# Two layers of triangle multiplication: masking the finished operands instead of the gates, and a step's stages spread over one more tick

## The reference

```python
# layer 0
z_norm = layer_norm(z, ln_w, ln_b)
m = mask[..., None]
a = (z_norm @ W_ap + b_ap) * sigmoid(z_norm @ W_ag + b_ag) * m
b = (z_norm @ W_bp + b_bp) * sigmoid(z_norm @ W_bg + b_bg) * m
z = z + (einsum('bikc,bkjc->bijc', a, b) @ W_z + b_z)
# layer 1, no mask
x = layer_norm(z, ln1_w, ln1_b)
left, right = sigmoid(x @ left1) * (x @ left2), sigmoid(x @ right1) * (x @ right2)
p = layer_norm(einsum('nsre,nkre->nske', left, right), ln2_w, ln2_b)
out = z + (p @ out_w) * sigmoid(x @ gate)
```

## The kernel before, in words

| stage | ticks | contents | us from the span's start |
|---|---|---|---|
| A | 54 | a z step each, from tick 6 on one half each (0 to 47) | 0 to 247 |
| B | 8 | two halves each (48 to 63), spill | 247 to 291 |
| C | 16 | contraction 0, the last 12 z steps (52 to 63) | 291 to 344 |
| D | 16 | an x step and two halves of layer 0 each | 344 to 447.8 |
| E | 16 | contraction 1 | 447.8 to 482 |
| F | 16 | as D | 482 to 582.7 |
| G | 16 | contraction 2 | 582.7 to 615 |
| H | 16 | an x step each | 615 to 689 |
| I | 16 | contraction 3 | 689 to 716 |
| J | 32 | an x step every second tick, two halves of layer 1 each | 716 to 838 |
| K | 16 | contraction 4 | 838 to 872 |
| L | 16 | a p step and two halves each | 872 to 944 |
| rest | | contraction 5, as L, contraction 6, 16 p steps, contraction 7, 16 p steps | 944 to 1225 |

## Time and profile before

### The profile page before, as it was taken

How to read it: one execution, slowest core, us unless ns; L and a number is a source line. 1 busy time by engine, 2 the same in 40 slices (tenths; PEclk the granted TensorE clock), 3 DMA queues, 4 the chain that set the end, 5 groups by cost and what they waited for, 6 DMA issues and landing times.

```text
span 1225.6 us, 26377 instructions
## 1 busy us (share of the span) xinstructions
PE 900.5 (73%) x9820; PEld 849.1 (69%) x9820; DVE 807.3 (66%) x1883; ACT 583.7 (48%) x834; POOL 690.2 (56%) x441
## 2 busy tenths in 40 slices
PE   1546555467867689676967888888998999956965
PEld 1445454467867579665955888888898999946854
DVE  4888898945658851888167347662597299089097
ACT  1566666653935443455334445553454355333333
POOL 2576777766658851888045213331486188178097
PEclk9876667787988989999988899999999999989989
DMA  2334357776876733665766425676486288866156
GB/s 71 110 106 130 110 146 233 225 237 237 293 218 200 211 103 100 190 196 175 245 210 182 137 78 175 204 260 243 127 305 205 81 293 285 260 219 224 44 190 206
DMA packets 173238, 228.72 MB, mean 187 GB/s; under 512 B 11064, under 2 KB 109624, under 8 KB 171064
## 3 DMA queue, kind: packets, MB, share of 16 engines
q1 hardware_dynamic: 173112, 227.04, 59.4%
HBM read 134.73 MB, written 92.27 MB: 185 GB/s over the span
## 4 chain that ended last, share of the span: by engine, by line
PE 28%; DVE 26%; POOL 19%; issue 17%; ACT 4%; DMA 3%; SPq 2%; DVEq 0%; POOLq 0%; ACTq 0%
PE bank L918 18%; POOL rstd L511 13%; DVE stats L762 7%; DVE xc L795 6%; POOL sig L504 5%; DVE lhs L745 3%; PE ps_w L948 3%; PE bank L902 2%; DVE xc L787 2%; PE bank L903 2%; DVE var L770 2%; POOL xc L523 2%; DMA chunk<-xt 1%; DVE rhs L745 1%; PE ps_x L959 1%
## 5 line engine op out<-in xcount | busy, mean ns | idle before, releaser
L511 POOL TENSOR_TENSOR rstd<-var,minus_half 128x8 f32<-128x8 f32 x192 | 377.3, 1966 | 375.1 <-DVE var L770 375.0
L918 PE MATMUL bank<-rhs,lhs 128*128 128x128 f32 x2048 | 245.6, 283 | 15.5 <-DVE rhs L745 9.0
L504 POOL TENSOR_TENSOR sig<-sig,masks 128x512 f32<-128x512 f32 x128 | 182.6, 1433 | 128.4 <-ACT sig L569 127.5
L569 ACT ACTIVATE sig<-bank 128x512 f32<-128x512 f32 x256 | 153.1, 598 | 212.0 <-PE bank L903 202.0
L918 PEld LDWEIGHTS bank<-rhs,lhs 128*128 128x128 f32 x2048 | 241.0, 198 | 16.5 <-DVE rhs L745 9.5
L959 PE MATMUL ps_x<-ident_b,split 128*128 128x128 bf16 x1024 | 101.1, 257 | 142.9 <-DVE split L802 142.8
L795 DVE TENSOR_TENSOR xc<-xc,rstd 128x504 f32<-128x504 f32 (+1 forms) x192 | 161.1, 839 | 62.3 <-POOL xc L523 35.0
L902 PE MATMUL bank<-w_lhs,chunk 128*128 128x128 bf16 x1024 | 157.1, 242 | 51.7 <-DVE lhs L745 37.9
L902 PE MATMUL bank<-w_rhs,chunk 128*128 128x128 bf16 x1024 | 158.7, 245 | 40.4 <-DVE rhs L745 29.6
L959 PEld LDWEIGHTS ps_x<-ident_b,split 128*128 128x128 bf16 x1024 | 78.0, 116 | 158.5 <-DVE split L802 134.6
L948 PE MATMUL ps_w<-w_out,opair 128*128 128x128 f32 x1024 | 152.0, 296 | 39.1 <-DVE split L809 35.4
(11 more groups left out here) (83 smaller groups left out, 1348.7 us busy)
## 6 DMA issues: line engine op xcount, KB each, us to landing
xt<-xt SPq DMA_DIRECT2D x96, 512.0 KB, 4.4
chunk<-xt SPq DMA_DIRECT2D x80, 512.0 KB, 4.4
xin<-in_x_dram SPq DMA_DIRECT2D x128, 256.0 KB, 3.0
x<-xin SPq DMA_DIRECT2D x64, 256.0 KB, 3.7
xin<-x SPq DMA_DIRECT2D x64, 256.0 KB, 3.9
out_dram<-xin SPq DMA_DIRECT2D x64, 256.0 KB, 3.2
spill<-lhs SPq DMA_DIRECT2D x8, 1024.0 KB, 6.4
chunk<-xcol SPq DMA_DIRECT2D x16, 512.0 KB, 4.0
```

What stands on the lines that cost most here:

```text
L504: g.tensor_tensor(sig[:, s], sig[:, s], table[:, other, first:first + COLS].unsqueeze(1).broadcast_to([P, C, COLS]), ALU.mult).then_inc(ma ...
L511: g.tensor_tensor(rstd[:, m % 2], var[:, m % 2], minus_half[:, :], ALU.pow).then_inc(rooted, 1)
L569: a.activation(sig[:, s], v[:, 0:C, :], ACT.Sigmoid).then_inc(gated, 1)
L918: last = mm(bank[:, n], operand["lhs"][:, kh, c, :], operand["rhs"][:, kh, c, :], start=kh == 0, stop=kh == HALVES - 1)
```

## The change

**Masks.** `mask_gate` is gone: ScalarE's gate goes straight to VectorE's make. In its place GpSimd multiplies finished operand tiles of half 0 (`mask_operand`, 48 operations of 128x512: 32 on rhs, one per tick from tick 22 on, then 16 on lhs with kh = 0, two per tick in B), and VectorE multiplies the rest in eight groups of 8 channels per contraction (`mask_group`): 8 operations of 128x1024 at contraction 0, 8 of 128x2048 at contraction 1 (lhs) and 8 of 128x2048 at contraction 2 (rhs). Contraction 0 waits for all 48 of GpSimd's, and each group of contractions 0, 1 and 2 for its own mask on VectorE. SyncE's spill of layer 0 waits for the masks of what it stores.

**Stages.** For z steps centre comes in the tick of the statistics, the root too, high one tick earlier, normalise stays one tick later; `lag` is 5, and in A gates and make of a half are one tick behind its project. For x steps normalise is two ticks behind the step's tick instead of one, low and turn_x three instead of two, xt_out four instead of three, its store five instead of four. For all steps variance follows statistics at once. The program has one tick fewer.

```diff
-    lag = 6
-    for t in range(54):
+    lag = 5
+    for t in range(53):
         tick(t if t < 52 else None, [t - lag] if t >= lag else [])
...
+def first_half(t):
+    return halves_at(t)[0] if len(halves_at(t)) == 2 else None
+def second_half(t):
+    return halves_at(t)[-1] if halves_at(t) else None
+POOL_MASKS = 3 * C // 4
+MASK_FIRST, MASK_TWO = 22, 54
+def pool_masks_at(t):
+    if MASK_FIRST <= t < MASK_TWO:
+        return [t - MASK_FIRST]
+    if MASK_TWO <= t < MASK_TWO + C // 8:
+        return [2 * C // 4 + 2 * (t - MASK_TWO), 2 * C // 4 + 2 * (t - MASK_TWO) + 1]
+    return []
+VECTOR_MASKS = {0: ("lhs", 1, 2), 1: ("lhs", 0, 2), 2: ("rhs", 0, 2)}
...
 # SyncE, spill
-                sp.wait_ge(made, after(2 * ((NEEDS[0] if layer == 0 else NEEDS[4])
-                                            - (0 if kh else CHUNKS // (2 if layer == 0 else 1))) - 1))
+                if layer == 0:
+                    if kh == 0:
+                        sp.wait_ge(masked_p, 2 * C // 4 + C // 16 * (part + 1))
+                    else:
+                        sp.wait_ge(masked_v, 2 * (part + 1))
...
 # GpSimd
+            def mask_operand(n):
+                kh, c = n // (C // 4) % 2, 4 * (n % (C // 4))
+                op, table = ("rhs", mask_kj) if n < 2 * C // 4 else ("lhs", mask_ki)
...
+                if c == 0:
+                    pool.wait_ge(made, after(CHUNKS * (n // (C // 4) + 1) - 1))
+                part = operand[op][:, kh, c:c + 4, :]
+                g.tensor_tensor(part, part, table[:, kh, 0:P].unsqueeze(1).broadcast_to([P, 4, P]),
+                                ALU.mult).then_inc(masked_p, 1)
...
+                for lag, kinds in ((0, "zp"), (1, "x")):
+                    s = step_at(t - lag)
+                    if s is not None and step(s)[0] in kinds:
+                        root(s)
+                        if centre_on_pool(s):
+                            centre(s)
...
+                for n in pool_masks_at(t):
+                    mask_operand(n)
...
 # ScalarE
+                if second_half(t - 1) is not None:
+                    gates(second_half(t - 1))
...
+                s = step_at(t - 1)
+                if s is not None and s < X_BASE:
+                    high(s)
...
 # VectorE
-                if layer == 0:
-                    dve.wait_ge(masked, after(h))
-                else:
-                    dve.wait_ge(gated, after(h))
+                dve.wait_ge(gated, after(h))
...
+            def mask_group(q, group):
+                op, low_kh, high_kh = VECTOR_MASKS[q]
+                table, half = (mask_ki, P * (q == 1)) if op == "lhs" else (mask_kj, P)
+                dve.wait_ge(made, after(2 * NEEDS[q] - 1))
+                part = operand[op][:, low_kh:high_kh, CG * group:CG * (group + 1), :]
+                v.tensor_tensor(part, part, table[:, low_kh:high_kh, half:half + P].unsqueeze(2).broadcast_to(
+                    [P, high_kh - low_kh, CG, P]), ALU.mult).then_inc(masked_v, 1)
...
+                if unit and second_half(t - 1) is not None:
+                    make(second_half(t - 1))
+                if unit and unit[0] in VECTOR_MASKS and unit[1] < GROUPS_C:
+                    mask_group(unit[0], unit[1])
+                for s in (due, begin):
+                    if s is not None:
+                        statistics(s)
+                        variance(s)
+                if not unit and second_half(t - 1) is not None:
+                    make(second_half(t - 1))
...
+                s = step_at(t - 2)
+                if s is not None and X_BASE <= s < P_BASE:
+                    normalise(s)
...
 # TensorE, first unit of a group
+                    if q == 0:
+                        pe.wait_ge(masked_p, POOL_MASKS)
+                    if q in VECTOR_MASKS:
+                        pe.wait_ge(masked_v, GROUPS_C * q + u // 2 + 1)
```

More of the change, by code:

```diff
@@ L494, in _ @@
                             base=0, pattern=[[-1, P]], channel_multiplier=1).then_inc(idents, 1)
[L496 to L501, removed]
-                    pool.wait_ge(ready, 1)
[L503 to L506, removed]
+            def mask_operand(n):
+                kh, c = n // (C // 4) % 2, 4 * (n % (C // 4))
+                op, table = ("rhs", mask_kj) if n < 2 * C // 4 else ("lhs", mask_ki)
+                if n == 0:
+                    pool.wait_ge(ready, 1)
+                if c == 0:
[3 more added lines that the diff above has]
+                                ALU.mult).then_inc(masked_p, 1)
             def root(m):
@@ L817, in _ @@
             for t in range(T_END):
-                before, now = halves_at(t - 1), halves_at(t)
                 start, ago = step_at(t), step_at(t - 1)
-                if ago is not None and X_BASE <= ago < P_BASE:
-                    statistics(ago)
+                unit = TICKS[t][2]
+                due = ago if ago is not None and X_BASE <= ago < P_BASE else None
                 if start is not None and not X_BASE <= start < P_BASE:
-                    statistics(start)
-                if len(before) == 2:
-                    make(before[1])
@@ L826, in _ @@
-                if ago is not None and X_BASE <= ago < P_BASE:
-                    variance(ago)
-                if start is not None and not X_BASE <= start < P_BASE:
-                    variance(start)
-                if ago is not None and not centre_on_pool(ago):
-                    centre(ago)
+                    begin = start
+                else:
+                    begin = None
+                if unit and second_half(t - 1) is not None:
+                    make(second_half(t - 1))
@@ new lines, in _ @@
+                if unit and unit[0] in VECTOR_MASKS and unit[1] < GROUPS_C:
[6 more added lines that the diff above has]
+                    make(second_half(t - 1))
+                s = step_at(t - 3)
+                if s is not None and X_BASE <= s < P_BASE:
+                    low(s)
@@ L832, in _ @@
+                if s is not None and s >= P_BASE:
+                    scale(s)
                 s = step_at(t - 2)
-                if s is not None and s < P_BASE:
+                if s is not None and s < X_BASE:
                     low(s)
+                for s in (due, begin if begin is not None and begin < X_BASE else None,
+                          ago if ago is not None and ago >= P_BASE else None):
+                    if s is not None and not centre_on_pool(s):
+                        centre(s)
@@ L842, in _ @@
-                if now:
-                    make(now[0])
-                if ago is not None and centre_on_pool(ago):
-                    normalise(ago)
+                if first_half(t) is not None:
+                    make(first_half(t))
                 if ago is not None and ago >= P_BASE and ago % 2 == 0:
@@ L976, in _ @@
             for t in range(T_END):
-                now = halves_at(t)
-                start, s2 = step_at(t), step_at(t - 2)
+                start = step_at(t)
+                due = start if start is not None and X_BASE <= start < P_BASE else None
+                late = step_at(t - 2) if step_at(t - 2) is not None and step_at(t - 2) >= P_BASE else None
                 unit = TICKS[t][2]
-                first = bool(now) and t > 0 and TICKS[t - 1][2] is not None
+                first = first_half(t) is not None and t > 0 and TICKS[t - 1][2] is not None
                 if unit:
```

94 lines of the change are left out of this document (43 added, 51 removed).

## The result

The changed kernel takes 1249.51 us (median of four runs, 1249.05 to 1251.89) against 1225.89 us before in the same measurements: a ratio of 1.0189, 95% interval 1.0152 to 1.0227. It is slower by 23.6 us, where 1143 us was forecast with a range of 1108 to 1195. The profiled execution has a span of 1250.1 us, 24.5 us more than before.

The account below looks back on a forecast made before the run. No engine was taken to bound the whole kernel; limits change by stage, several being loops of waits. Terms -27 - 2 + 7 - 48 + 9 - 11 - 13 = -85 from 1227.4 gave 1142.4, stated as 1143 us, range 1108 to 1195.

Parts of the forecast that it names:

- step A: First stage, 45 ticks: only VectorE's work remains, 3.6 us a tick, 4.05 with a mask; 27 us gained, ends 8 and 40.
- The mask in A: GpSimd's operand mask in 30 ticks of the first stage: holds VectorE by nothing or 1.07 us; 4.05 us a tick taken.
- L and later: Late stages: variance before make, scale before centre, no operation added; change 0 us, ends -4 and +4.
- C: Stage with contraction 0: 7.4 us wait at its head, early rounding -3, VectorE masks +3; sum +7, ends +3 and +12.
- B's small gain: 8 ticks of two halves: gate masks leave the loop, SyncE's spill waits for GpSimd's masks; 2 us gained, ends 0 and 6.
- H and J: Later step stages: H 3.9 us a tick, from 74.0 us, 11 gained; J 6.8 us a step, 13 gained.
- D and F: Two stages of 16 ticks: root loop cut, VectorE's queue bounds, 5.0 us a tick; 24 us gained each, ends 13 and 30.
- E and G: Contractions 1 and 2: first VectorE mask of 2.3 us and late transposes show; +4.5 us each, ends +3 and +7.
- Case 2 (transfers): Rival: transfers or TensorE's order take over, D and F at 5.9 us a tick; 1195 us, chance 0.15.
- case 3 (roots exclude VectorE): Rival: root and two-input VectorE operations exclude each other, D tick 5.7 us; 1188 us, chance 0.10.
- The slower case: Rival: TensorE's granted clock falls in D and F, 7.5 us a tick, 16 us lost in each; 1248 us, chance 0.05.
- 0.92 for faster: Whole kernel: chance 0.92 that it becomes faster by more than 0.5% (6 us).

Follow-up runs that it names:

- e1: Changed kernel with the z steps' rounding on ScalarE (high) put back to its old tick, two behind the step: 1167.49 us, ratio to before 0.952.
- e7: Kernel before with only the masks changed (GpSimd's 48 and VectorE's 24 operand masks replace the masked gates), no stage moved: 1149.08 us, ratio 0.9358.
- e2: Changed kernel with high kept in its early tick but moved behind xt_out and col_out in ScalarE's queue: 1181.00 us, ratio to before 0.9618.
- e9: e6 with each operand mask of stage A waiting on GpSimd for the normalise of the step one tick back: 1114.71 us, ratio 0.908.
- e11: e4 with normalise of the p steps that GpSimd centres put back behind the second make: 1230.58 us, ratio to before 1.0028.
- e8: e1 without VectorE's 16 masks at contractions 1 and 2 (not applied to those operand halves): 1159.77 us.
- e5: Changed kernel with both repairs, the z rounding as in e1 and the p steps' variance and centre as in e4: 1147.28 us, ratio 0.9349.
- e4: Changed kernel with, in p steps, variance behind the make and centre before scale again: 1226.53 us, ratio to before 1.0000.
- e6: e5 with GpSimd's last two operand masks ahead of step 52's root and centre, and lhs, kh = 0 spills two ticks later: 1135.54 us, ratio 0.926.
- e10: Operand masks, z steps and halves of A in old order, x steps spread, p steps reordered by stage, spills two ticks later: 1099.59 us, ratio 0.8952.

## Why the prediction was wrong

**Where it failed: step A.** The prediction said "What is left is VectorE's own work: 0.99 + 4 x 0.6 (make, low, centre, normalise) = 3.4, with waits 3.6". VectorE's work was right (e1 and e7: 3.50 and 3.39 us); that nothing but it was left was wrong. I had followed each semaphore back one tick and found it free, but not the order of ScalarE's queue, and the prediction names no loop through it: high now stands ahead of xt_out and col_out, and these ahead of the next gate. With e1's ticks A would have gained 12.5 us; it lost 57.6. e1 (one move undone, 82 us back, the loop gone from the chain) and e2 (the same tick, other place, 68 us back) show both the cause and its place.

**The mask in A.** The text gave "nothing" and "1.07" as ends and took the middle, 4.05 us a tick. In the changed kernel the slower loop hid all but 0.27 of it; once that was gone (e1) it was the full 1.07 (4.57): GpSimd has no other work, so the mask always starts right behind the root, at the very time when normalise is ready. An average between two ends was no estimate here, since the order fixes which of them holds. e9 and e7 show that it can be made to be almost nothing.

**L and later**, "No operation is added ... 0, ends -4 and +4": +17.3. Nothing was added, but the earlier variance starts GpSimd's root, centre and add earlier, into VectorE's normalise and spread copy: 0.85 and some 0.6 us lost each time (rows of L above). I looked at who waits for variance and not at what its successors on GpSimd would meet. And one move, that of normalise, was missed altogether (e11).

**C**: 7.4 us for the head were 8.8, since the root there took 2.49 and not 1.6. The three us that high ahead of the drain was to give back did not come: with high put back (e1) contraction 0 lasts 48.7 us, with high ahead 48.8. B's small gain was eaten by SyncE's wait, 14.3 us of it, which the text named as a risk and did not price.

**H and J.** H's sum began from 74.0 us, which holds 6.4 us of contraction 3. The tick was forecast well (3.9 said, 60.5 / 16 = 3.8 measured), but from the 68.4 us that H really took it gives 7.9 us and not 11. J is another matter: 6.8 us a step said, 118.0 / 16 = 7.4 measured. Root, centre and normalise have left its chain, and another loop stands there (changed kernel):

```profile
783.55 0.69 DVE xin L817
...
784.76 0.89 DVE stats L804 x4
785.67 0.17 DVE var L812
785.84 0.61 DVE lhs L778
...
786.59 0.25 PE bank L955
```

The mix of a step releases the add, statistics and variance follow, the make stands behind them, and the next projection needs the bank that this make frees. From 740 to 840 us TensorE waits 12.5 us in all for it, 0.9 us a step. The sum had TensorE's 6.4 us as the floor and no price for this wait. No run moved that make.

**What held.** D and F: 5.0 us a tick said, 4.7 measured in the middle and 5.0 and 4.8 in the mean; 24 us each said, 24.9 and 24.4 measured from contraction to contraction. VectorE is the bound, with no transfer in its way, although the DMA share rose from 0.62 to 0.81. Case 2 (transfers) and case 3 (roots exclude VectorE) are out for D and F. E and G: +9 said, and e8 puts the two sets of masks at 7.7. H with I and J with K gave 8.5 and 7.9 us where 11 and 13 were said: right in kind, too large in size. With the two mistakes repaired and nothing else, the kernel takes 1147 us (e5) where 1143 was forecast; part of that agreement is chance: A with e1's ticks gains 12.5 us where 27 was said and C costs 12 where 7 was said, while the p stages in the order of e4 and D and F with their contractions gave more than was said.

**The rivals.** The slower case was the clock: right side, wrong mechanism. TensorE's granted clock did fall, but in A, and not as the cause (e1 has its ticks of 3.5 us at the same clock); in D it rose from 0.89 to 0.98. Its 1248 us beside the measured 1249.5 is no merit. And 0.92 for faster was far too sure. A change that rewrites the order on four queues has many loops, and the sum had checked only those that existed before.

What stays open: whether moving J's make gives back its 0.9 us a step, and why the hole in B did not close fully in e6.

## What to carry to other kernels

When a stage is moved in one engine's queue, write down the loop for every operation that now stands behind it, engine by engine in queue order, and not only the semaphores: a wait costs whatever stands behind it. Where VectorE and GpSimd share work, ask at which VectorE operation each GpSimd operation will start; here the same mask cost 0 (e7), 0.37 (e9) or 1.07 us (e1) a tick by its place alone, and adding a wait to move it gained 21 us. When an order change is large, take its parts one at a time: of this one the masks gained 77 us, the spreading of the x steps some 40 more, and a single early rounding lost 82.

## What the runs showed of the hardware that I had not expected

A root (128x8, power) that is running held no VectorE operation: low starts 0.37 us into it and takes 0.67 (the tick of D above), and in the kernel before all 95 normalises and 64 lows that began beside a running root took 0.67 to 0.69. A 128x512 mask holds a VectorE operation with two SBUF inputs to its end, 1.75 us instead of 0.68. Statistics, with one input, and makes, with one input from PSUM, took their plain time beside a mask.

The other way round a root is held. In the kernel before, the 44 that began with VectorE idle took 1.63 or 1.64 us, the 63 that began while a centre (two SBUF inputs) was running 1.94 to 2.54. In the changed kernel the 76 that began beside a make took 1.64 or 1.65. So the 2.54 us of the earlier trace rows are, by these rows, 1.64 and a hold of 0.9, and by moving variance ahead of the make the change also shortened the root of D.

The Trainium skill (SBUF — State Buffer, section Who interferes with whom) says that a VectorE instruction with two SBUF inputs and a GpSimd one that reads SBUF exclude each other for the whole instruction; that fits the masks, the centre against normalise and the roots that are held, but not a VectorE operation that begins beside a root. The spread copy of bf16, which has one SBUF input and so is not of this kind, was held by the residual add as well (1.28 instead of 0.68).

TensorE's granted clock in A was 0.57 in the changed kernel, 0.68 before, 0.94 in e7 and 0.96 in e10. It did not set the tick, and the tick alone did not set it: between 98 and 140 us e5 and e6 had the same ticks of 4.57 us, e5 at a granted clock of 0.50 and e6 at 0.82, and from 45 to 98 us e1 ran at 0.58 with ticks of 3.50, e7 at 0.94 with 3.39. What differs with the clock is TensorE's busy time for nearly the same number of matmuls: 116.7 us (x1069) in A of the changed kernel, 108.5 (x1069) before, 73.5 (x1074) in e10.
